# Handing over from the first attention to the first experts: order of residual and selection, ten one-hots on ScalarE, unread products

## What is computed

```python
x = x + tanh(g_xattn[0]) * L0_xattn(layernorm(x), ctx, ...)
x = x + tanh(g_ffn[0]) * L0_ffn(layernorm(x), ...)   # 8 experts, 2 chosen per token
x = x + tanh(g_xattn[1]) * L1_xattn(layernorm(x), ctx, ...)
x = x + tanh(g_ffn[1]) * L1_ffn(layernorm(x), ...)   # 15 experts, 3 chosen, one shared

# L0_ffn:
router_logits = einsum('bth,eh->bte', x, router_w)
topk_values, topk_indices = top_k(router_logits, 2)
topk_weights = softmax(topk_values)
h1 = gelu(einsum('bth,efh->btef', x, w1) + b1)
out = einsum('btef,ehf->bteh', h1, w2) + b2          # only the chosen experts are needed
```

## Time and profile before

| | |
|---|---|
| median of three runs | 1222.9 us |
| profiled execution, own time | 1222.04 us |
| its span | 1220.3 us |
| TensorE busy | 1164.6 us, 95% |
| VectorE, ScalarE, GpSimd busy | 596.4, 478.2, 390.7 us |
| mean granted clock of TensorE | 0.987 |

### The profile page before, as it was taken

One profiled execution on the slowest core, in us unless ns is written; L12 is line 12 of the kernel. 1 busy time (PEld: TensorE's weight loads), 2 busy tenths in 40 slices (PEclk: granted clock), 3 DMA queues, 4 the chain that ended last, 5 costly groups with the idle time before them and its releaser, 6 DMA issues. The chain is left out here.

```text
span 1220.3 us, 29213 instructions
## 1 busy us (share of the span) xinstructions
PE 1164.6 (95%) x11433; PEld 899.5 (74%) x11433; DVE 596.4 (49%) x1437; ACT 478.2 (39%) x1130; POOL 390.7 (32%) x411
## 2 busy tenths in 40 slices
PE   6999999977999999998999999999998999999998
PEld 4767777755999999975566666666665589999975
DVE  5777777775211101047867667567656511122126
ACT  3545555522332333224544454454454133322221
POOL 3666766642222222131001011011021245555510
PEclk9999999977999999999999999999999999999999
DMA  6001011405999998732021001000000469999964
GB/s 186 22 27 38 26 36 34 136 8 183 386 335 319 329 333 321 278 104 55 2 87 33 14 20 33 14 9 9 2 15 17 164 213 357 356 350 351 343 221 163
DMA packets 64392, 180.93 MB, mean 148 GB/s; under 512 B 10176, under 2 KB 36608, under 8 KB 55808
## 3 DMA queue, kind: packets, MB, share of 16 engines
q1 hardware_dynamic: 55088, 156.40, 37.5%
q0 software_dynamic: 8064, 22.03, 5.0%
q10 hardware_dynamic: 1104, 0.64, 0.2%
HBM read 163.11 MB, written 15.93 MB: 147 GB/s over the span
## 5 line engine op out<-in xcount | busy, mean ns | idle before, releaser
L2344 ACT ACTIVATE ex_hT<-kept_psum,ex_w 128x128 f32<-128x128 f32 x464 | 132.2, 368 | 295.0 <-PE kept_psum L2399 169.7
L2399 PE MATMUL kept_psum<-ex_xT,ex_w 128*128 128x128 f32 x1856 | 222.5, 276 | 0.0
L2399 PEld LDWEIGHTS kept_psum<-ex_xT,ex_w 128*128 128x128 f32 x1856 | 215.6, 193 | 0.1
L2410 PE MATMUL kept_psum<-ex_w,ex_hT 128*128 128x256 f32 x928 | 213.9, 379 | 0.0
L2306 DVE TENSOR_TENSOR ex_yt<-kept_psum,ex_b 128x256 f32<-128x256 f32 x84 | 35.7, 425 | 352.9 <-PE kept_psum L2410 352.9
L2410 PEld LDWEIGHTS kept_psum<-ex_w,ex_hT 128*128 128x128 f32 x928 | 170.1, 190 | 19.7
L2272 POOL DMA_INDIRECT ex_results<-ex_yt,ex_to_row x84 | 82.8, 986 | 254.7 <-DVE ex_yt L2306 254.7
L1273 ACT ACTIVATE at_probs<-kept_psum 120x800 f32<-120x800 f32 (+2 forms) x128 | 101.1, 841 | 77.0 <-PE kept_psum L1455 77.0
L1097 DVE TENSOR_REDUCE at_negmax<-kept_psum 100x2 f32<-100x722 f32 x128 | 115.4, 902 | 0.0
L568 ACT ACTIVATE at_probs<-kept_psum 120x800 f32<-120x800 f32 (+1 forms) x96 | 80.0, 836 | 73.6 <-PE kept_psum L691 73.5
L410 DVE TENSOR_REDUCE at_negmax<-kept_psum 120x8 bf16<-120x800 f32 (+1 forms) x96 | 90.6, 985 | 23.7 <-PE kept_psum L682 23.3
(11 more groups left out here) (256 smaller groups left out, 1688.6 us busy)
## 6 DMA issues: line engine op xcount, KB each, us to landing
ex_w<-in_pack_in SPq DMA_DIRECT2D x32, 1028.0 KB
ex_w<-in_pack_out SPq DMA_DIRECT2D x32, 1024.0 KB
ex_w<-in_pack_in SPq DMA_DIRECT2D x52, 514.0 KB
ex_w<-in_pack_out SPq DMA_DIRECT2D x52, 512.0 KB
at_ctx<-in_ctxT SPq DMA_DIRECT2D x31, 361.0 KB, 3.7
ex_normed<-ex_xhat SPq DMA_DIRECT2D x16, 200.0 KB
ex_w<-ex_results SPq DMA_DIRECT2D x6, 400.0 KB
ex_sw<-in_L_ffn_sW SPq DMA_DIRECT2D x2, 1024.0 KB
```

Of the source, the lines that this page charges most:

```text
L2344: last = act.activation(hT[t % N][:, c, :], ps_h[:, (t * U + u) % N, i * P:(i + 1) * P], ACT.Gelu, bias=w1[t % N][:, B1 + c:B1 + c + 1])
L2399: last = pe.matmul(ps_h[:, (t * U + u) % N, i * P:(i + 1) * P], w1[t % N][:, c * ff + f:c * ff + f + P], xT[t % N][:, c, :], start=(c == 0 ...
L2410: last = pe.matmul(ps_y[:, t % N, 0:D], hT[t % N][:, c, :], w2[t % N][:, c * D:(c + 1) * D], start=(c == 0), stop=(c == FC - 1))
```

## The change

Six things are changed; the arithmetic result stays the same.

1. In step t = 16 of `attend0` VectorE does `residual(14)` before the selection of the first part, not after it.
2. `select` takes the choices to make: the first choice in step 16, the second (with the mask) in step 17 after the moments of pair 7. `lanes` of the first part moves from step 17 to step 18, and TensorE's first `rank_up` behind the `late_tensor` of step 17.
3. Of the 32 one-hots of the first experts ten are made by ScalarE: for the last four batches of the first part and the last one of the second, for both choices. ScalarE takes |lane - position| (Abs) and then Relu(token - 128 token x that). VectorE counts `lane_known` up when the lanes stand. ScalarE makes the first eight after its loop, ahead of the keys, and the last two between keys 3 and 4.
4. `scale_tokens` on ScalarE makes the factor -128 x token, once.
5. `keep_warm`: eight products that nothing reads, four before each of two shifts of batch 15, into the bank that batch 14's values use next.
6. Twelve more such products after the table.

```diff
@@ attend0, vector
         for t in range(B + 4):
             if t == B:
                 prep.normed(dve, PAIRED - 2)
-                prep.route.select(dve, 0)
             if on(t - 2):
                 residual(t - 2)
+            if t == B:
+                prep.route.select(dve, 0, range(1))
...
             if t == B + 1:
+                prep.route.select(dve, 0, range(1, 2))
+            if t == B + 2:
                 prep.route.lanes(dve, 0)
-            if t == B + 2:
                 prep.route.in_lanes(dve, 0)
@@ attend0, scalar
+            if t == B:
+                prep.route.scale_tokens(act)
             if t > B:
                 late_scalar(act, prep, psum, t)
+        prep.route.in_lanes_act(act, 0)
@@ attend0, tensor
+        def keep_warm(bank, n):
+            for _ in range(n):
+                pe.matmul(bank[:, 0:P], ident[:, :], wk[:, 0, 0:P], start=True, stop=True)
...
+            if t == LAST:
+                keep_warm(into("sum", LAST - 1), 4)
             if on(t):
                 shift(t, 0, 0)
...
+            if t == LAST:
+                keep_warm(into("sum", LAST - 1), 4)
             if on(t):
                 shift(t, 1, 0)
...
+            if t > B:
+                late_tensor(pe, prep, psum, t)
             if t == B + 1:
                 prep.route.rank_up(pe, 0)
-            if t > B:
-                late_tensor(pe, prep, psum, t)
@@ routing
+        def by_act(i):
+            return 0 if shared else (4, 1)[i]
...
-            for k in range(top):
+            for k in ks:
...
+            if ks[-1] < top - 1:
+                return
...
         def in_lanes(dve, i):
+            dve.sem_inc(lane_known, 1)
             for k in range(top):
-                for b in range(*SPLIT[i]):
+                for b in range(SPLIT[i][0], SPLIT[i][1] - by_act(i)):
...
+        def scale_tokens(act):
+            act.wait_ge(consts_set, 7)
+            act.activation(by_token[:, :], tok[:, :], ACT.Copy, scale=float(-P)).then_inc(token_ready, 1)
+
+        def in_lanes_act(act, i):
+            act.wait_ge(token_ready, 1)
+            act.wait_ge(lane_known, i + 1)
+            for k in range(top):
+                for b in range(SPLIT[i][1] - by_act(i), SPLIT[i][1]):
+                    n = counted[0]
+                    counted[0] += 1
+                    need(act, shown, n - 1)
+                    act.activation(off_lane[:, n % 2, :], minus_lanes[0:T, :], ACT.Abs, bias=lane_of[:, k, b:b + 1], scale=-1.0).then_inc(apart, 1)
+                    act.wait_ge(apart, n + 1)
+                    act.activation(in_lane[:, k * B + b, :], off_lane[:, n % 2, :], ACT.Relu, bias=tok[:, b:b + 1],
+                                   scale=by_token[:, b:b + 1]).then_inc(shown, 1)
@@ tabulate
                     pe.wait_ge(lanes_ready, i * top + k + 1)
+                    need(pe, shown, sum(top * by_act(j) for j in range(i)) + (k + 1) * by_act(i))
@@ main, scalar
             if not shared:
-                early.scalar(act, range(2, KC * early.AHEAD))
+                early.scalar(act, range(2, 4))
+                route.in_lanes_act(act, last)
+                early.scalar(act, range(4, KC * early.AHEAD))
@@ main, tensor
             route.tabulate(pe)
             if early is not None:
                 early.tensor_done(pe)
+                for _ in range(12):
+                    pe.matmul(ps_t[:, 1, 0:P], ident[:, :], early.wa[:, 0, 0:P], start=True, stop=True)
```

## The result

The changed kernel took 1226.42 us (median of 22 executions, 1222.32 to 1229.43), the kernel before, measured beside it, 1223.28 us. One of the 22 executions of before took 1943.26 us; the others lie between 1222.01 and 1227.40. The ratio is 1.0022 with a 95% interval of [1.0014, 1.0029]: 1.7 to 3.5 us slower. That is less than 0.5%, but on the other side than forecast, and 1226.42 lies outside the range of 1217 to 1225.5.

A forecast was written before the change was run, and what follows sets the result against it. TensorE, 95% busy, was taken as the bound. Terms +1.4 - 0.8 + 0.9 + 0 = 1.5 us off 1222.04 gave 1220.5, with the median's 0.9 1221.4, stated as 1221.0; range 1217 to 1225.5.

The forecast's parts named there:

- What bounds the kernel: From first expert tile to second attention: TensorE, 95% busy; bringing the tile forward shortens the whole run by as much.
- Part 1: Attention's end: residual in front and selection in halves start batch 15's projection 2.4 us earlier, normalization ends 2.1 us earlier.
- The eight products, taken at 0: Before two shifts of batch 15: between 1.4 us won and 1.5 to 2 us lost, taken as 0.
- the bad case: At batch 15: 6.8 us of half clock hits values and projections, some 1.5 to 2 us lost.
- VectorE does not profit: Chunk 2 at batch 15: VectorE takes its maxima after GpSimd's sums, so faster scores on TensorE bring nothing.
- Part 2: Table passage: ScalarE one-hots at 0.8 us each (0.55 to 0.95); table ends at 289.0 against 290.44, 1.4 us won.
- The clock in the new gap: TensorE idle 1.3 us between keys 1 and 2 may lower the clock: 0 to 4.9 us, 0.8 lost taken.
- The twelve products: After the table, ahead of the first gather: clock may hold into the first tile, 0 to 1.7 us, 0.9 won taken.
- No table load: ScalarE: Abs and Relu need no load; the rival, 1.28 us per load and 1224 to 1225 in all, had chance 0.04.
- The base: Whole run: 1222.04 us profiled, shown median 1222.9; the sum's 1221.4 was given as 1221.0.
- ScalarE as the bound: Key 0's eviction waits for eight one-hots, keys 2 to 5 run at half clock: 1225, at worst 1226; chance 0.18.

The follow-up runs named there:

- order_only: The kernel before with only the new order (residual first, selection in halves); all one-hots on VectorE, no unread products; ratio 0.9998.
- after_mid: The changed kernel with the shared expert's two 1 MB weight loads issued one batch later; ratio to the kernel before 1.0007.
- no_unread: The changed kernel without its 20 unread products, ten one-hots still on ScalarE; ratio to the kernel before 0.9999.
- few_hold: The changed kernel with six one-hots on ScalarE, no unread products at batch 15, 20 after the table and 4 after the first turn; ratio to before 1.0011.
- small_before: The kernel before plus 40 small unread f16 products after the table, 80 TensorE rows more; ratio 1.0016.
- after_late: The changed kernel with the shared expert's two 1 MB weight loads issued two batches later; ratio to the kernel before 1.0011.
- after_bias: The changed kernel with the load of the shared expert's first bias issued one batch later; ratio to the kernel before 1.0029.
- shifted_before: The kernel before plus 20 unread one-column products at TensorE's start, 80 rows more; ratio 1.0049.
- gather_only: The kernel before plus only the twelve unread products after the table, 48 TensorE rows more; ratio 1.0008.
- hold_clear: few_hold plus 8 small unread f16 products after the table, 112 TensorE rows more than the kernel before; ratio to before 1.0001.
- hold_bias: few_hold with the load of the shared expert's first bias issued one batch later; ratio to the kernel before 1.0003.
- warm_only: The kernel before plus only the eight unread products of batch 15, 32 TensorE rows more; ratio 1.0004.
- few_warm: The changed kernel with six one-hots on ScalarE, keeping the eight unread products but not the twelve; ratio to the kernel before 1.0001.
- before_bias: The kernel before with the load of the shared expert's first bias issued one batch later; ratio 0.9999.

## Why the prediction was wrong, step by step

- **What bounds the kernel.** That time won in the passage is kept to the end was right as far as the passage's waits go. It left out that more instructions can cost time later, which no wait of before shows. This is the step that failed: "nothing later absorbs it" was true as far as the waits go, but something later was added, 2.2 us in the trace of after.
- **Part 1, 2.1 us earlier.** Right in its mechanism: 266.25 against 266.0 for the projection, 1.7 us instead of 2.1 at the turn of the last pair (order_only). In after itself only 0.5 (keys at 277.42 against 277.92), with the clock's fall behind the eight products.
- **The eight products, taken at 0.** The prediction named the mechanism, that the fall is only put off and hits values and projections, and priced it at 1.5 to 2 us at worst, then took 0. In the trace of after it was 1.2 us: 267.43 against 266.25. The stretch behind the fall was 6.8 us long, as in the bad case. In after_mid, with the same code, it was a gain of 1.4, so a term of 0 between the two was no bad middle, but its range was missing from the sum. One reading in it was wrong: "VectorE does not profit". In after VectorE takes the maxima of chunk 2 at 255.91 instead of 257.04, and last_chunk starts at 258.57 instead of 260.17; that gain is then lost to the fall.
- **Part 2, one-hots at 0.8 us.** 0.82 measured. They start at 276.9 instead of 275.3, because everything stands 1.6 us later than summed (with the eight products at their bad case), and so key 2 comes at 284.25 instead of 282.45. The gap between the keys was forecast at 1.3 and is 1.35. The table ended at 290.25, not 289.0. The rule that the prediction set against this part, from the Trainium skill, page "ScalarE: Activation LUTs", section "Rules for kernel authors", that simple functions belong on VectorE, came out right for eight in a row: 0.227 us against 0.82, and the table is 1.0 us later with ten on ScalarE than with none. It did not come out for six, where ScalarE was idle otherwise: 288.23 against 289.70 at the table. At the end neither shows in the time (0.9999, 1.0000, and 0.9998 with none).
- **The clock in the new gap, 0.8 lost.** In after nothing was lost: the 16 rows took 5.10. In no_unread, where the gap is 2.24, it was 1.7. Both lie between the bounds given.
- **The twelve products, 0.9 won.** Nothing measurable. From the first hidden tile to the second it is 5.42 us in after and 5.26 in before. The term was a middle between 0 and 1.7, taken against the trace's own warning of 1.6 and 0.7 us idle; measured 1.84 and 0.71. In few_hold 24 products left 0.68 us of idle time, and the clock held; no number between was tried.
- **The price of 80 more TensorE rows, not in the sum at all.** 2.2 us in the rest of after; 2.0 us in small_before by its time. Of the 2.2, 1.2 net is the stop at row 11897: 1.72 us, less the 0.52 that it is in before. An instruction packet is late behind the weight loads, and with 80 rows more TensorE reaches the end of its stock before it comes; moving the weight loads removes the stop. Of the 0.4 at 910, 0.23 is a stop of the same kind, 1.3 us after the end of a packet, but with no other transfer in the 5 us before it, so these loads have no part in it. It is also in after_late, after_mid, after_bias, small_before and shifted_before, and in gather_only with 48 rows and hold_clear with 112. The 0.25 at 566 and the -0.2 at 1214 stand in no_unread too, without added rows; the small steps near 1030 and 1087 not in after_late. What makes these was not found.
- **No table load**: right, and as the Trainium skill says on the same page, "ScalarE: Activation LUTs", in "Table sets: the hidden batching unit".
- **The base.** 1226.42 - 1221.0 = 5.4 us. 0.8 of it is the base: 0.4 rounded down at the end of the sum, 0.4 between the 1222.9 of three runs and the 1223.28 of 22. The passage is 1.3 (1.5 forecast, 0.2 in the trace of after: 1.2 lost with the eight products and 0.9 not won with the twelve, against 0.8 of clock not lost), the rest of the span 2.2. The last 1.1 is the difference between what the two traces show (1224.08 - 1222.04 = 2.0) and what the medians do (3.1), and the traces cannot account for it. (By the ratio of 1.0022 the difference is 2.7, not 3.1.)

That the time stays within 0.5% was right, and most of the chance lay on it. The range was too narrow above by 0.9 us: none of its cases had a cost outside the passage. The size of the miss is in part luck: in a trace like that of after_mid the passage would have given 2.9 us and not 0.2. No rival of the prediction describes what happened; the nearest, ScalarE as the bound, shows in no_unread (the keys at half clock) and was worth 1.0 us at the table and nothing at the end.

## What to carry to other kernels

Unread products that filled only part of a gap moved the clock's fall into what ran next, with a gain in some executions and a loss in others; those that filled nearly all of it (few_hold) kept the clock up. With such a change, one trace of the passage isn't enough. And added instructions are not free even where their engine is idle: compare the two traces behind the changed place too, and where an engine stops on "issue", look for its instruction packets and for large loads at that moment. A gain ahead of a stretch that waits or runs at half clock should be followed to the first step behind it before it is counted.

## What the runs showed of the hardware

- An instruction packet of 16,384 bytes was 2.35 us late behind weight loads at 294 GB/s and TensorE stopped for 1.72 us (after); with the loads moved that packet was on time, and another was 3.7 us late behind the moved loads, without a stop (after_late).
- In eight traces TensorE stopped at the same count of its rows, 11895 to 11901, for 0.25 to 1.96 us, and went on 1.2 to 1.5 us after the packet's record ended. The long stops came with 80 to 96 more rows; with 0 to 48 the stop was 0.52 us or less, with 112 to 167, and with 96 in hold_bias, there was none.
- With the same code in the passage, the clock of TensorE was low for 6.8, 3.4 or 0 us at batch 15 (after, after_bias, after_mid), worth up to 2.7 us at the second hidden tile.
- Before an Abs or Relu on ScalarE no table is loaded in this kernel; an Abs of 100 x 128 with one pointer operand takes 0.39 us and a Relu with two 0.49, one behind the other 0.82 a pair.
- In some profiled executions of kernels that are the same there (order_only, warm_only, gather_only, few_warm, hold_clear, before_bias, after_bias), TensorE's clock is also low for 3.4 or 6.8 us near 32 us, which shifts all that follows by up to 3.8 us. Single executions of one kernel spread over several us (after 1222.32 to 1229.43); how much of it this makes was not measured.
